# Convolution of a decoder layer: blocks next to the diagonal as three split products, equal pairs squared on ScalarE, the pair products of a unit in two halves

## The chip, the cores and the metric

The kernel runs on one NeuronCore of a Trainium2 chip. Its five engines (TensorE, VectorE, ScalarE, GpSimd, SyncE) run programs of their own and meet at semaphores. The metric is device time in microseconds, lower is better. The kernel before takes 1985.09 us (median of three runs, 1984.59 to 1986.24).

## The reference, cut to what matters

A decoder layer for x of 16 x 256 x 512: attention with a sliding window, then a long convolution mixed with a context, then a sum of eight factor matrices. The change lies in the second part:

```python
kv = jnp.einsum('bhil,bhjl->bijhl', k_, v_)          # k_ and v_ are both the context here
y = irfft(rfft(kv, 1024) * rfft(ssm_kernel, 1024))[..., :512]   # causal convolution along l = 512
out = y + kv * D
out = jnp.einsum('bijhl,bhil->bjhl', out, q_)        # q_: the normalised rows of x
```

Here b runs over 16 batches, h over 32 heads, i and j over the 8 rows of a head, and l over the 512 positions. As k_ and v_ are the same tensor, kv is symmetric in i and j: 36 products of pairs, 8 of them (i = j) squares.

## The kernel before, in words

The convolution is a product with a lower triangular Toeplitz matrix of 512 x 512 for each head (in the kernel's layout the block at distance d under the diagonal is columns d*128 to d*128+127 of a table of shifted taps). One unit is one head and one of two groups of eight batches (BG = 8), 64 units in all (NCU). Its moving matrix has NY = 36 x 8 = 288 columns in each of four chunks of 128 positions (KD = 4). So a unit has ten blocks (c, d) with d <= c: four with c - d = 0, three with c - d = 1, two with 2, one with 3, where c - d picks the chunk of pair products and d the block of taps.

The names: `kk` holds the context of a unit (8 rows for each of 8 batches, four of the rows a second time), loaded by SyncE, two buffers. `kv` holds the 288 products, two buffers; `kv_hi` and `kv_lo` are its rounded part and the rest, `tap_hi` and `tap_lo` the same for the taps. `qs` holds the queries, `y` the result in PSUM (two halves of four banks), `terms` and `res` the sums over i. Units 6 to 57 are "split" (`ALONE = 6`): in them the four blocks with c = d are computed as three matmuls (hi*hi, hi*lo, lo*hi, line 1244) in the reduced float32 form; all other blocks are one float32 matmul in the source, which stands in the trace as two instructions (line 1246).

What each engine does for units in the convolution part, in program order and with lines of the profile:

- SyncE: `kk` of unit u (L1105) waits for the pair products of unit u - 2 (`kv_ready`). The taps of a head (L1114, and L1117 for the split forms) are loaded once for the two units of a head, into one of two buffers, and wait for `conv_done` of the head two before.
- GpSimd, round u: the pair products of unit u + 2 in two operations (L1159, all four chunks of distances 0 to 3; L1161, the pairs at distance 4), behind `kk_landed` and `conv_done` of unit u; then the last sum of unit u - 1 (L1183), then `kv_lo` of unit u + 2 (L1176).
- ScalarE, round u: the queries of unit u + 1 (L1201, L1202), the cast to `kv_hi` of unit u + 2 (L1172), then the result of unit u - 1 back into the big buffer (L1207).
- TensorE: unit u (L1244, L1246) waits for taps, `kv_ready`, `kv_lo_ready`, and for `one_added` of unit u - 2, because the result goes to the same half of PSUM.
- VectorE: unit u (L1280, L1283, L1285, L1290, then the dependent sums L1298, L1301, L1304 that end in `one_added`) waits for `qs_ready`, `res_ready` of unit u - 2 and `conv_done` of unit u.

All orders are written out in the source; there is no scheduler.

## Time and profile before

| what | us |
|---|---|
| median of three runs | 1985.09 |
| the profiled execution's own time | 1984.65 |
| its span | 1982.9 |
| attention part (until about) | 1545 |
| convolution units 6 to 57, first to last VectorE start | 1578.07 to 1825.03 |
| last part (factors), from about | 1857 |

The page gives busy time by engine; the views used further below are the chain of work that ended last, the engines in order of time, the groups of instructions of a stretch, and the busy time by stretches. TensorE's granted clock was 0.996 of full over the whole span. A line of the chain says on which engine and line the end of the program hung in that piece of time.

### The profile page before, as it was taken

How to read it: one execution, taken by the hardware profiler on the slowest of the kernel's cores; microseconds unless marked ns; L12 is line 12 of the kernel's file. 1: busy time of each engine (PE TensorE's matmuls, PEld its weight loads, DVE VectorE, ACT ScalarE, POOL GpSimd, SP SyncE). 2: the span in 40 equal slices, each digit the busy share in tenths (PEclk: the TensorE clock that was granted, in tenths of full speed). 3: DMA queues.
4: the chain of work that ended last, by engine and by line, in shares of the span. 5: the costliest groups of instructions: out<-in, count | busy, mean ns of one | idle time of the engine just before them, and what ended most of it. 6: DMA issues, size and time to landing. Idle time of an engine off the chain costs nothing.

```text
span 1982.9 us, 45446 instructions
## 1 busy us (share of the span) xinstructions
PE 1930.0 (97%) x15708; PEld 1610.9 (81%) x15708; DVE 1547.7 (78%) x4948; ACT 954.6 (48%) x3534; POOL 866.7 (44%) x1000
## 2 busy tenths in 40 slices
PE   6899999999999999999999999999999999999899
PEld 6688888888888888888888888888886788887687
DVE  6777777777777777777777777777777799999887
ACT  4554555555555555555555555555554233333333
POOL 4444334333433343333333333333332588887554
PEclk9999999999999999999999999999999999999999
DMA  6147211111112122121111111111105655554333
GB/s 216 44 121 148 69 54 55 64 54 55 55 55 73 47 97 76 55 80 71 55 55 54 55 55 54 55 56 64 55 33 200 169 118 118 115 113 100 109 141 121
DMA packets 75828, 167.59 MB, mean 85 GB/s; under 512 B 7120, under 2 KB 19536, under 8 KB 75472
## 3 DMA queue, kind: packets, MB, share of 16 engines
q1 hardware_dynamic: 67008, 147.84, 23.7%
q0 software_dynamic: 3840, 8.39, 2.3%
q10 hardware_dynamic: 4752, 8.46, 1.1%
q8 instruction: 127, 2.08, 0.4%
q14 instruction: 101, 0.83, 0.1%
HBM read 114.08 MB, written 50.58 MB: 83 GB/s over the span
## 4 chain that ended last, share of the span: by engine, by line
PE 85%; DVE 9%; issue 2%; ACT 2%; POOL 1%; DMA 1%; DVEq 0%; SPq 0%; ACTq 0%; POOLq 0%
PE banks L542 22%; PE banks L604 18%; PE banks L581 9%; PE banks L557 9%; PE banks L1246 7%; PE banks L567 6%; PE banks L535 5%; PE banks L1474 5%; PE banks L1244 3%; DVE terms L1280 1%; ACT pr L681 1%; DVE banks L1298 1%; DVE banks L1290 1%; PE banks L492 1%; DVE terms L1301 1%
## 5 line engine op out<-in xcount | busy, mean ns | idle before, releaser
L681 ACT ACTIVATE pr<-pr,mx 128x128 f32<-128x128 f32 x1024 | 399.1, 391 | 354.3 <-DVE mx L905 354.3
L763 POOL TENSOR_TENSOR m<-m,rope_sb 128x512 f32<-128x512 f32 x160 | 206.5, 1291 | 512.7 <-ACT m L668 512.7
L542 PE MATMUL banks<-xTh,wh 128*128 128x256 f32 x1280 | 375.8, 294 | 2.3 <-DVE xTl L865 1.4
L542 PE MATMUL banks<-xTl,wh 128*128 128x256 f32 x1280 | 362.5, 283 | 0.0
L542 PE MATMUL banks<-xTh,wl 128*128 128x256 f32 x1280 | 362.0, 283 | 0.0
L914 DVE TENSOR_TENSOR den<-ac,es 128x4 f32<-128x4 f32 x256 | 51.6, 202 | 253.4 <-ACT es L684 253.3
L542 PEld LDWEIGHTS banks<-xTh,wh 128*128 128x128 f32 x1280 | 245.6, 192 | 4.2 <-issue 1.8
L542 PEld LDWEIGHTS banks<-xTl,wh 128*128 128x128 f32 x1280 | 246.0, 192 | 0.0
L542 PEld LDWEIGHTS banks<-xTh,wl 128*128 128x128 f32 x1280 | 245.2, 192 | 0.0
L1246 PE MATMUL banks<-kv,tap 128*128 128x288 f32 x864 | 238.4, 408 | 2.1 <-DMA tap<-padded_taps 1.5
L905 DVE CUSTOM_DVE_ANT_0 pr<-banks,mask_sb 128x128 f32<-128x128 f32 x1024 | 234.8, 283 | 0.2
L780 POOL TENSOR_TENSOR sk<-mx,sink_sb 128x4 f32<-128x4 f32 x256 | 59.8, 233 | 383.4 <-DVE mx L905 383.3
L581 PE MATMUL banks<-pT,vv 128*64 128x256 f32 (+1 forms) x2048 | 223.1, 339 | 1.7 <-DVE oTl L936 1.7
L604 PE MATMUL banks<-woh,oTh 128*128 128x512 f32 x512 | 220.5, 431 | 0.4 <-DVE x L949 0.4
L668 ACT ACTIVATE m<-banks,bqk_sb 128x256 f32<-128x256 f32 x320 | 134.2, 470 | 163.7 <-PE banks L542 163.4
L557 PE MATMUL banks<-kT,qT 32*128 32x128 f32 (+1 forms) x4096 | 203.8, 335 | 3.2 <-DVE mx L905 2.4
L581 PEld LDWEIGHTS banks<-pT,vv 128*64 128x64 f32 x2048 | 124.7, 136 | 97.8 <-issue 43.2
L604 PE MATMUL banks<-woh,oTl 128*128 128x512 f32 x512 | 200.9, 392 | 0.0
L604 PE MATMUL banks<-wol,oTh 128*128 128x512 f32 x512 | 200.8, 392 | 0.0
L881 DVE SCALAR_TENSOR_TENSOR m<-banks,bqk_sb,rope_sb 128x256 f32<-128x256 f32 x320 | 139.8, 478 | 77.5 <-ACT m L668 72.3
L919 DVE TENSOR_TENSOR pr<-pr,rden 128x512 f32<-128x512 f32 x256 | 188.2, 735 | 8.8
L681 ACT ACTIVATION_READ_ACCUMULATOR pr<-pr,mx 128x1 f32 x1024 | 191.3, 187 | 0.0
(120 smaller groups left out, 4192.4 us busy)
## 6 DMA issues: line engine op xcount, KB each, us to landing
kk<-in_ctxt SPq DMA_DIRECT2D x64, 192.0 KB, 3.6
x_in<-in_x SPq DMA_DIRECT2D x16, 512.0 KB, 3.5
xt_split<-xTh SPq DMA_DIRECT2D x16, 512.0 KB, 2.7
xt_split<-xTl SPq DMA_DIRECT2D x16, 512.0 KB, 4.0
xb<-in_x SPq DMA_DIRECT2D x16, 512.0 KB, 4.2
factors<-in_factors POOLq DMA_DIRECT2D x8, 1024.0 KB, 8.6
x_part_rows<-x SPq DMA_DIRECT2D x16, 512.0 KB, 3.0
xTh<-xt_split SPq DMA_DIRECT2D x16, 512.0 KB, 4.8
```

Source lines behind the costliest of these rows:

```text
L542: last = pe.matmul(bank[:, h * T:(h + 1) * T], w[:, n, c, h * P:(h + 1) * P], a[:, s, c, :], start=(c == 0 and i == 0), stop=(c == KD - 1 ...
L557: last = pe.matmul(sP[:, r, t * P:P + 2 * t * P], qT[rr, p % 2, h, t * P:(t + 1) * P], kT[rr, kslot, h, 0:(t + 1) * P], start=(h == 0), st ...
L567: last = pe.transpose(pP[:, (2 * a + t) * P:(2 * a + t + 1) * P], pr[:, (2 * p + 2 + j) % 4, a, t * P:(t + 1) * P], id_sb[:])
L581: last = pe.matmul(vP[a * HD:(a + 1) * HD, k * P:T], vv[:, (u // 4) % 2, k, g * HD:(g + 1) * HD], pT[:, s, a, 2 * k * P:2 * P + k * P], st ...
L604: last = pe.matmul(oP[:], a[:, o, c, t * P:(t + 1) * P], w[:, c, :], start=(c == 0 and n == 0), stop=(c == NO - 1 and n == 2))
L668: last = act.activation(m2[:, s, 1 - half], bank[:, half * T:(half + 1) * T], ACT.Identity, bias=bqk_sb[:, y.sweep, i, half:half + 1])
L681: act.activation(pr[:, s, a, cols], pr[:, s, a, cols], ACT.Exp, bias=mx[:, s, i:i + 1], scale=-1.0, accum_out=ac[:, s, i:i + 1])
L763: pool.tensor_tensor(m2[:, s], m2[:, s], rope_sb[:, 1 if i == 0 else 0, 1:3], ALU.mult).then_inc(sin_ready, 1)
L881: last = dve.scalar_tensor_tensor(m1[:, s, half], bank[:, half * T:(half + 1) * T], bias[:, half:half + 1], tab[:, 0], ALU.add, ALU.mult)
L905: last = dve.tensor_tensor_reduce(pr[:, s, a, t * P:(t + 1) * P], sP[:, 2 * j + a, 2 * t * P:(2 * t + 1) * P], mask_sb[:, t * P:(t + 1) * ...
L919: dve.tensor_tensor(quarters, quarters, rden[:, s].unsqueeze(2).broadcast_to([P, 2 * NT, P]), ALU.mult).then_inc(pn_ready, 1)
L1246: last = pe.matmul(y[:, s, c, 0:NY], tap[:, k, block], kv[:, s, c - d, :], start=(d == 0), stop=(d == c))
```

## The change

In split units the three blocks with c - d = 1 are computed in three split matmuls too. For this `kv_hi` and `kv_lo` hold chunks 0 and 1 instead of chunk 0 alone, so the cast on ScalarE and the subtraction on GpSimd have 576 columns instead of 288. Chunks 0 and 1 of `kv` are then read by no matmul. The pair products of a split unit are made in four operations on GpSimd, two for chunks 0 and 1 (`half` 0) and two for chunks 2 and 3 (`half` 1), and the pairs at distance 0 are left out there; ScalarE makes them as squares of `kk`, in two operations. Half 0 of unit u + 2 waits for no `conv_done` where unit u is split. The whole taps that are loaded for a split head shrink from 384 to 256 columns. `pT` of the attention part moves into the space of the pairs, which doubles.

GpSimd, the products of unit 8 and what follows them, before (kk the context, kv the products, res the last sum of unit 5):

```order
L1159 TENSOR_TENSOR kv<-kk 128x4x256 [waits conv_done,kk_landed0]
L1161 TENSOR_TENSOR kv<-kk 128x4x32
L1183 TENSOR_TENSOR res<-terms 128x256 [waits res_placed,one_added]
L1176 TENSOR_TENSOR kv_lo<-kv,kv_hi 128x288 [waits kv_hi_ready]
L1159 TENSOR_TENSOR kv<-kk 128x4x256 [waits conv_done,kk_landed1]
```

and in the changed kernel:

```order
L1189 TENSOR_TENSOR kv<-kk 128x2x192 [waits kk_landed0]
L1191 TENSOR_TENSOR kv<-kk 128x2x32
L1189 TENSOR_TENSOR kv<-kk 128x2x192 [waits conv_done,kk_landed0]
L1191 TENSOR_TENSOR kv<-kk 128x2x32
L1229 TENSOR_TENSOR res<-terms 128x256 [waits res_placed,one_added]
L1222 TENSOR_TENSOR kv_lo<-kv,kv_hi 128x576 [waits kv_hi_ready]
```

The two operations of 1024 and 128 elements a partition became four of 384 and 64, the first two without `conv_done`; `kv_lo` doubled in size.

ScalarE, the round that casts `kv_hi` of unit 8, before:

```order
L1201 COPY qs<-queries 128x4x64 [waits q_landed1,terms_ready]
L1202 COPY qs<-queries 128x4x32
L1172 CAST kv_hi<-kv 128x288 [waits kv_ready]
L1207 COPY queries<-res 128x4x8x8 [waits q_landed0,res_ready]
L1201 COPY qs<-queries 128x4x64 [waits q_landed0,terms_ready]
```

and in the changed kernel:

```order
L1250 COPY qs<-queries 128x4x64 [waits q_landed1,terms_ready]
L1251 COPY qs<-queries 128x4x32
L1205 ACTIVATE kv<-kk 128x2x64 [waits kv_lo_ready,kk_landed0]
L1217 CAST kv_hi<-kv 128x576 [waits conv_done,kv_first_ready,kv_square_ready]
L1205 ACTIVATE kv<-kk 128x2x64 [waits conv_done]
L1256 COPY queries<-res 128x4x8x8 [waits q_landed0,res_ready]
```

Two squares (ACTIVATE) stand around the cast, which is twice as wide and now waits for the first half of the products, the first squares and `conv_done` instead of `kv_ready`.

TensorE, the start of unit 6 (output chunks 0, 1 and a part of 2), before:

```order
L1244 MATMUL banks<-kv_hi,conv_tap_hi 128x288 [waits kv_lo_ready,one_added,kv_ready,tap_landed0]
L1244 MATMUL banks<-kv_lo,conv_tap_hi 128x288
L1244 MATMUL banks<-kv_hi,conv_tap_lo 128x288
L1246 MATMUL banks<-kv,tap 128x288
L1244 MATMUL banks<-kv_hi,conv_tap_hi 128x288
L1244 MATMUL banks<-kv_lo,conv_tap_hi 128x288
L1244 MATMUL banks<-kv_hi,conv_tap_lo 128x288
L1246 MATMUL banks<-kv,tap 128x288 x2
```

and in the changed kernel:

```order
L1294 MATMUL banks<-kv_hi,conv_tap_hi 128x288 [waits kv_equal_ready,kv_lo_ready,one_added,kv_ready,tap_landed0]
L1294 MATMUL banks<-kv_lo,conv_tap_hi 128x288
L1294 MATMUL banks<-kv_hi,conv_tap_lo 128x288
L1294 MATMUL banks<-kv_hi,conv_tap_hi 128x288
L1294 MATMUL banks<-kv_lo,conv_tap_hi 128x288
L1294 MATMUL banks<-kv_hi,conv_tap_lo 128x288
L1294 MATMUL banks<-kv_hi,conv_tap_hi 128x288
L1294 MATMUL banks<-kv_lo,conv_tap_hi 128x288
L1294 MATMUL banks<-kv_hi,conv_tap_lo 128x288
L1297 MATMUL banks<-kv,tap 128x288
```

The single float32 block of output chunk 1 became three split matmuls, and one of the two float32 blocks of output chunk 2 as well. Over a unit, 12 split and 6 float32 matmuls became 21 and 3.

The diff:

```diff
--- before.py
+++ after.py
@@ -99,7 +99,7 @@
         self.fsum = self.tables + 6 * T + 2 * GS * HD
         self.probs = self.fsum + KD * D
         self.pairs = self.probs + 8 * T
-        words = self.pairs + 4 * NY
+        words = self.pairs + 8 * NY
         ctx.enter_context(nc.sbuf_tensor("arena", [P, words], F32))
         self.base = nc.sbuf_base - 4 * words
         self.id_sb = ctx.enter_context(nc.sbuf_tensor("id_sb", [P, P], F32))
@@ -157,7 +157,7 @@
     ac = sb("ac", [P, 4, 2 * NT])
     den = sb("den", [P, 4, 2 * NT])
     rden = sb("rden", [P, 4, 2 * NT])
-    pT = sb("pT", [P, 2, 2, SK])
+    pT = space.at("pT", space.pairs, 2, 2, SK)
     xb = sb("xb", [P, NT, D])
     x1 = sb("x1", [P, NT, D])
     x1n = xn
@@ -1046,8 +1046,8 @@
     terms = space.at("terms", space.moving + 5632, 2, KD, 5 * 8 * BG)
     tap_hi = space.at("conv_tap_hi", space.probs, 2, D, dt=F32R)
     tap_lo = space.at("conv_tap_lo", space.probs + 2 * D, 2, D, dt=F32R)
-    kv_hi = space.at("kv_hi", space.pairs, 2, NY, dt=F32R)
-    kv_lo = space.at("kv_lo", space.pairs + 2 * NY, 2, NY, dt=F32R)
+    kv_hi = space.at("kv_hi", space.pairs, 2, 2, NY, dt=F32R)
+    kv_lo = space.at("kv_lo", space.pairs + 4 * NY, 2, 2, NY, dt=F32R)
     big = space.queries
     y = space.banks[:].rearrange("p (s c) n -> p s c n", s=2)
 
@@ -1056,6 +1056,9 @@
     kk_landed = [sem(f"kk_landed{i}") for i in range(2)]
     tap_landed = [sem(f"tap_landed{i}") for i in range(2)]
     kv_ready = sem("kv_ready")
+    kv_first_ready = sem("kv_first_ready")
+    kv_equal_ready = sem("kv_equal_ready")
+    kv_square_ready = sem("kv_square_ready")
     kv_hi_ready = sem("kv_hi_ready")
     kv_lo_ready = sem("kv_lo_ready")
     qs_ready = sem("qs_ready")
@@ -1102,6 +1105,8 @@
     def load_contexts(sp, u):
         bg, h, s = where(u)
         wait(sp, kv_ready, u - 1)
+        if split(u - 2):
+            sp.wait_ge(kv_equal_ready, u - 2 - ALONE + 1)
         sp.dma_start(kk[:, s], ctx_in[bg, h]).then_inc(kk_landed[s], 16)
 
     def load_taps(sp, u):
@@ -1110,7 +1115,7 @@
             return
         if g > 1:
             sp.wait_ge(conv_done, opening[g - 1])
-        whole = D - P if split(u) else D
+        whole = D - 2 * P if split(u) else D
         sp.dma_start(tap[:, g % 2, 0:whole], diagonals(0, h, whole)).then_inc(tap_landed[g % 2], 16)
         if split(u):
             for i, part in ((1, tap_hi), (2, tap_lo)):
@@ -1148,19 +1153,57 @@
             for b in {4: (12, 13), 5: (14,), 6: (15,)}.get(u, ()):
                 load_queries(sp, b)
 
+    def contexts(u):
+
+        k0 = kk[:, u % 2, :, 0:8, :].rearrange("p c i b -> p c (i b)")
+        row = k0.ap[1][0]
+
+        def later(first, apart, count, half):
+            c = 2 * half if half is not None else 0
+            n = KD if half is None else 2
+            return bass.AP(tensor=k0.tensor, offset=k0.offset + c * row + first * BG,
+                           ap=[list(k0.ap[0]), [row, n], [BG, count], [1, 8 * BG]])
+
+        return k0, later
+
     def pairs(pool, u):
         s = u % 2
         pool.wait_ge(kk_landed[s], 16 * (u // 2 + 1))
         wait(pool, conv_done, u - 1)
         n = 8 * BG
-        k0 = kk[:, s, :, 0:8, :].rearrange("p c i b -> p c (i b)")
-        row = k0.ap[1][0]
-        shifted = bass.AP(tensor=k0.tensor, offset=k0.offset, ap=[list(k0.ap[0]), [row, KD], [BG, 4], [1, n]])
+        k0, later = contexts(u)
         pool.tensor_tensor(kv[:, s, :, 0:4 * n].rearrange("p c (d n) -> p c d n", d=4),
-                           k0.unsqueeze(2).broadcast_to([P, KD, 4, n]), shifted, ALU.mult)
+                           k0.unsqueeze(2).broadcast_to([P, KD, 4, n]), later(0, 1, 4, None), ALU.mult)
         pool.tensor_tensor(kv[:, s, :, 4 * n:NY],
                            kk[:, s, :, 0:4, :].rearrange("p c i b -> p c (i b)"),
                            kk[:, s, :, 4:8, :].rearrange("p c i b -> p c (i b)"), ALU.mult).then_inc(kv_ready, 1)
+
+    def unequal_pairs(pool, u, half):
+
+        s, c = u % 2, slice(2 * half, 2 * half + 2)
+        pool.wait_ge(kk_landed[s], 16 * (u // 2 + 1))
+        if half or not split(u - 2):
+            pool.wait_ge(conv_done, u - 1)
+        n = 8 * BG
+        k0, later = contexts(u)
+        pool.tensor_tensor(kv[:, s, c, n:4 * n].rearrange("p c (d n) -> p c d n", d=3),
+                           k0[:, c].unsqueeze(2).broadcast_to([P, 2, 3, n]), later(1, 1, 3, half), ALU.mult)
+        pool.tensor_tensor(kv[:, s, c, 4 * n:NY],
+                           kk[:, s, c, 0:4, :].rearrange("p c i b -> p c (i b)"),
+                           kk[:, s, c, 4:8, :].rearrange("p c i b -> p c (i b)"),
+                           ALU.mult).then_inc(kv_ready if half else kv_first_ready, 1)
+
+    def equal_pairs(act, u, half):
+
+        s, c = u % 2, slice(2 * half, 2 * half + 2)
+        if not half:
+            act.wait_ge(kk_landed[s], 16 * (u // 2 + 1))
+        if not half and split(u - 2):
+            act.wait_ge(kv_lo_ready, u - 2 - ALONE + 1)
+        else:
+            act.wait_ge(conv_done, u - 1)
+        last = act.activation(kv[:, s, c, 0:8 * BG], kk[:, s, c, 0:8, :].rearrange("p c i b -> p c (i b)"), ACT.Square)
+        last.then_inc(kv_equal_ready if half else kv_square_ready, 1)
 
     def first_pairs(pool, u):
         if u == 0:
@@ -1168,12 +1211,15 @@
         pairs(pool, u)
 
     def pairs_high(act, u):
-        act.wait_ge(kv_ready, u + 1)
-        act.copy(kv_hi[:, u % 2], kv[:, u % 2, 0, :]).then_inc(kv_hi_ready, 1)
+        equal_pairs(act, u, 0)
+        act.wait_ge(kv_first_ready, u - ALONE + 1)
+        wait_apart(act, conv_passed, (kv_square_ready, u - ALONE + 1), (conv_done, u - 1))
+        act.copy(kv_hi[:, u % 2], kv[:, u % 2, 0:2, :]).then_inc(kv_hi_ready, 1)
+        equal_pairs(act, u, 1)
 
     def pairs_low(pool, u):
         pool.wait_ge(kv_hi_ready, u - ALONE + 1)
-        pool.tensor_tensor(kv_lo[:, u % 2], kv[:, u % 2, 0, :], kv_hi[:, u % 2].bitcast(F32),
+        pool.tensor_tensor(kv_lo[:, u % 2], kv[:, u % 2, 0:2, :], kv_hi[:, u % 2].bitcast(F32),
                            ALU.subtract).then_inc(kv_lo_ready, 1)
 
     def last_sum(pool, u):
@@ -1184,7 +1230,10 @@
 
     def gpsimd(pool):
         for u in range(NCU):
-            if u + 2 < NCU:
+            if split(u + 2):
+                unequal_pairs(pool, u + 2, 0)
+                unequal_pairs(pool, u + 2, 1)
+            elif u + 2 < NCU:
                 pairs(pool, u + 2)
             if u > 0:
                 last_sum(pool, u - 1)
@@ -1231,6 +1280,7 @@
         pe.wait_ge(kv_ready, u + 1)
         if split(u):
             pe.wait_ge(kv_lo_ready, u - ALONE + 1)
+            pe.wait_ge(kv_equal_ready, u - ALONE + 1)
         wait(pe, one_added, u - 1)
         for c in range(KD):
             if u == 1 and c == KD - 1:
@@ -1239,9 +1289,10 @@
                 pe.wait_ge(x1t_evac, 2 * B)
             for d in range(c + 1):
                 block = slice(d * P, (d + 1) * P)
-                if c == d and split(u):
+                if c - d < 2 and split(u):
                     for n, (a, b) in enumerate([(tap_hi, kv_hi), (tap_hi, kv_lo), (tap_lo, kv_hi)]):
-                        last = pe.matmul(y[:, s, c, 0:NY], a[:, k, block], b[:, s], start=(d == 0 and n == 0), stop=(n == 2))
+                        last = pe.matmul(y[:, s, c, 0:NY], a[:, k, block], b[:, s, c - d], start=(d == 0 and n == 0),
+                                         stop=(d == c and n == 2))
                 else:
                     last = pe.matmul(y[:, s, c, 0:NY], tap[:, k, block], kv[:, s, c - d, :],
                                      start=(d == 0), stop=(d == c))
```

## Rows read from the trace of the kernel before

**Rows 1.** The page: span, then busy time, share of the span and instructions.

```profile
span 1982.9 us, 45446 instructions
...
PE 1930.0 (97%) x15708; PEld 1610.9 (81%) x15708; DVE 1547.7 (78%) x4948; ACT 954.6 (48%) x3534; POOL 866.7 (44%) x1000
```

**Rows 2.** Busy us by engine in stretches, granted clock, DMA share, GB/s.

```profile
core 0: us, PE busy (x) PEld busy (x) DVE busy (x) ACT busy (x) POOL busy (x), PEclk, DMA share, GB/s
...
1574.00:1578.00 4.00, 4.00 (x16) 3.22 (x16) 0.36 (x1) 1.66 (x4) 3.43 (x4) 0.69 0.47 105
1600.00:1650.00 50.00, 48.66 (x249) 40.16 (x248) 47.16 (x73) 19.52 (x43) 42.75 (x43) 1.00 0.48 114
```

**Rows 3.** Chain that ended last, 1601 to 1622 us: start, duration, what.

```profile
1602.21 0.63 PE banks L1244 x3
1602.85 0.49 PE banks L1246 x2
1603.34 0.39 PE banks L1244 x3
...
1606.55 0.41 PE banks L1244 x3
...
1607.08 1.23 DVE terms L1280
...
1611.75 0.14 issue
1611.89 0.63 PE banks L1244 x3
```

**Rows 4.** Groups, 1600 to 1820 us: shapes, count | busy, mean ns | idle before.

```profile
...
L1159 POOL TENSOR_TENSOR kv<-kk 128x1024 f32<-128x1024 f32 x46 | 103.8, 2257 | 33.0 <-PE banks L1244 33.0
...
L1176 POOL TENSOR_TENSOR kv_lo<-kv,kv_hi 128x288 fp32r<-128x288 f32 x46 | 36.9, 802 | 0.0
...
L1183 POOL TENSOR_TENSOR res<-terms 128x256 f32<-128x256 f32 x46 | 33.7, 732 | 0.0
...
L1161 POOL TENSOR_TENSOR kv<-kk 128x128 f32<-128x128 f32 x46 | 21.1, 460 | 0.0
...
L1172 ACT CAST kv_hi<-kv 128x288 fp32r<-128x288 f32 x46 | 19.9, 432 | 123.9 <-POOL kv L1161 123.9
...
L1202 ACT COPY qs<-queries 128x128 f32<-128x128 f32 x46 | 18.9, 411 | 0.0
```

**Rows 5.** GpSimd in order of time, one unit: start, duration, what.

```profile
1602.05 2.26 POOL L1159 TENSOR_TENSOR kv<-kk 128x1024 f32<-128x1024 f32 x1 [0.51 <-PE banks L1244]
...
1605.36 0.81 POOL L1176 TENSOR_TENSOR kv_lo<-kv,kv_hi 128x288 fp32r<-128x288 f32 x1
1607.09 2.25 POOL L1159 TENSOR_TENSOR kv<-kk 128x1024 f32<-128x1024 f32 x1 [0.92 <-PE banks L1244]
```

**Rows 6.** VectorE in order of time: first op of four units, idle before.

```profile
1578.07 1.23 DVE L1280 TENSOR_TENSOR terms<-banks,qs 128x1024 f32<-128x1024 f32 x1 [3.71 <-PE banks L1244]
...
1582.65 1.22 DVE L1280 TENSOR_TENSOR terms<-banks,qs 128x1024 f32<-128x1024 f32 x1
...
1587.74 1.23 DVE L1280 TENSOR_TENSOR terms<-banks,qs 128x1024 f32<-128x1024 f32 x1 [0.43 <-PE banks L1244]
...
1825.03 1.22 DVE L1280 TENSOR_TENSOR terms<-banks,qs 128x1024 f32<-128x1024 f32 x1 [0.45 <-PE banks L1244]
```

**Rows 7.** SyncE's queue from 1600 us, and the landing of L1105's 64 loads.

```profile
1602.78 0.43 SPq L1117 DMA_DIRECT2D conv_tap_lo<-padded_taps  x1
1604.74 5.37 SPq L1105 DMA_DIRECT2D kk<-in_ctxt  x2
...
DMA to landing us min/median/max: 2.1/3.6/7.4
```

**Rows 8.** TensorE in order of time: the first split unit's start.

```profile
1571.52 0.40 PE L1244 MATMUL banks<-kv_hi,conv_tap_hi 128*128 128x288 f32 x1 [1.98 <-DMA conv_tap_lo<-padded_taps]
```

**Rows 9.** GpSimd at the end of the attention part.

```profile
1516.01 2.25 POOL L1159 TENSOR_TENSOR kv<-kk 128x1024 f32<-128x1024 f32 x1
...
1518.64 2.71 POOL L1159 TENSOR_TENSOR kv<-kk 128x1024 f32<-128x1024 f32 x1
```

## The prediction

> **What bounds the kernel now.** I read the page first. TensorE is busy for 97% of the span, VectorE for 78% [rows 1]. That mean says nothing of the stage that changes, so I asked for stretches. Between 1600 and 1650 us, inside the split units, TensorE is busy 48.66 of 50 us, VectorE 47.16, GpSimd 42.75, ScalarE 19.52, at a granted clock of 1.00 [rows 2]. Three engines are nearly full, so which one ends a unit has to be read from the chain.
>
> The chain [rows 3] alternates. A TensorE unit starts at 1602.21, VectorE's unit on its result at 1607.08, and the next TensorE piece on the chain at 1611.89, after 0.14 us of issue behind VectorE's end. That TensorE unit is two units later, since it waits for the PSUM half that VectorE has just given back. So two units take 1611.89 - 1602.21 = 9.68 us, or 4.84 a unit: 4.87 from TensorE's start to VectorE's (matmuls and handoff) plus 4.81 from VectorE's start to TensorE's (VectorE's unit, 4.67, and the 0.14). The VectorE starts of units 6 and 57 give the same from afar: (1825.03 - 1578.07) / 51 = 4.842 us [rows 6].
>
> Neither engine alone takes as long. VectorE's starts at 1578.07 and 1582.65 are only 4.58 apart, back to back without a wait, and the next, at 1587.74, comes after 5.09 us, 0.43 of it waiting for TensorE [rows 6]. So VectorE by itself could run a unit in about 4.59, and the loop through both is what costs 4.84.
>
> **The change, part by part.**
>
> *TensorE.* A unit loses three float32 blocks and gains three split triples. On the chain a float32 block (two instructions) takes 0.49 and a triple 0.39 to 0.41 away from the unit's start [rows 3]. The 0.63 at the start of a unit is a triple with the pipeline filling, and that is paid once in either kernel. The gain is 3 x (0.488 - 0.398) = 0.27 us a unit, where 0.488 and 0.398 are the middles of these rows. Bounds: 3 x (0.49 - 0.39) = 0.30 above. Below, if every triple cost the 0.63, 3 x (0.49 - 0.63) = -0.42; I take 0.27, since the triples inside the unit are the nearest rows, and there one already follows a float32 block each time. One more semaphore is waited for at the unit's start, but the last to arrive is still VectorE's.
>
> *The loop.* A TensorE unit stands once in a loop of two units, so the period falls by half of that: (9.684 - 0.27) / 2 = 4.707 us a unit. VectorE's own 4.59 lies below, so it doesn't take over. Between the VectorE starts of units 6 and 57 lie 51 periods: 51 x 0.135 = 6.9 us. Unit 6 itself starts when its taps have landed, behind 1.98 us of idle TensorE [rows 8]; it stands on the chain in full, so its 0.27 comes on top. Sum on TensorE and VectorE: -7.2 us.
>
> *GpSimd.* This is the engine that gets work. Before, a round is four operations of 1024, 128, 256 and 288 elements, mean 2257, 460, 732 and 802 ns [rows 4]. From the first two a rate follows: (2257 - 460) / 896 = 2.006 ns an element, with 0.203 us fixed. A round now has two of 384 elements (0.203 + 0.770 = 0.973 each), two of 64 (0.331 each), the last sum (0.732) and `kv_lo` of 576 (0.802 + 288 x 2.006 ns = 1.380). That is 4.72 us of durations. They overlap a little: before, four operations of 2.26 + 0.46 + 0.74 + 0.81 = 4.27 run from 1602.05 to 1606.17, in 4.12 [rows 4, 5], 0.05 for each joint. Six joints give 4.72 - 0.30 = 4.42. The lower bound is this 4.42. The upper is no overlap and a handoff of 0.13 exposed (the chain's TensorE piece ends at 1606.96 [rows 3], GpSimd starts at 1607.09 [rows 5]) at one of its waits: 4.85. I take 4.45, because the durations in these rows are steady and GpSimd now starts half 0 of the next unit ahead of `conv_done`, so that the handoff falls in a time when it has work. 4.45 is below 4.707, so GpSimd follows with 0.26 us to spare. Its `kv_lo` ends about 0.13 + 0.97 + 0.33 + 0.73 + 1.38 - 0.15 = 3.4 us after `conv_done` of unit u and is needed 4.7 after it, so a late round costs nothing unless it is late every time.
>
> [...]
>
> *ScalarE.* A round gains two squares of 128 elements and 288 more columns of cast. The rows give 432 ns for a cast of 288 and 411 for a copy of 128 [rows 4]; at most the additions are 0.43 + 2 x 0.41 = 1.25 us, at least 0.5 (a cast at half the rate and the squares hidden in overlaps). The engine is busy 19.52 of 50 us [rows 2], 1.9 a unit, so 3.1 at the most of 4.7. Cast and last squares are done by 0.13 + 0.86 + 0.41 = 1.4 us after `conv_done`, and GpSimd comes to `kv_lo` only about 2.0 after it. Behind the waiting cast are queued the second squares, the result of the unit before and the queries of the one after next; the last are due in two units. I cost it at nothing. If that cover went, GpSimd's `kv_lo` would move by the same amount, and 1.3 us of slack lie behind it.
>
> *SyncE and the loads.* `kk` of unit u + 2 may be issued when half 1 is done, about 1.3 us after `conv_done` instead of 2.7 (1604.74 against 1602.05 [rows 5, 7]). The new need is 3.3 us after the next `conv_done`, a period earlier than before less that. Lead before: 2 x 4.84 - 2.7 = 7.0; lead now: 4.7 + 3.3 - 1.3 = 6.7 us. Landing takes 3.6 in the median and 7.4 at worst [rows 7]; it now follows the taps (last issue 1602.78 + 0.43) at once rather than 1.5 us later, so it will take longer than the median. The worst row, if it came every time, would cost 0.7; I take 0. The taps are 128 columns shorter, a gain of nothing to 0.2 us at unit 6.
>
> *Start.* Unit 7's products begin late in any case, and its round is 0.3 us longer (4.42 against 4.12). It is not on the chain. I charge 0.2.
>
> *Sum.* -7.2 + 0.2 = -7.0 us against the profiled execution's own time, 1984.65, that is 1977.65. That execution is 0.44 below the median of the runs, so the forecast for the median is 1978.1.
>
> **The rivals.**
>
> *A. GpSimd ends the unit, but below 4.84.* If overlaps and handoffs come out near the upper bound, the period is 4.72 to 4.84 instead of 4.707: 4.78 gives 51 x 0.062 = 3.2 us saved, 1981.9. For it: GpSimd is busy 42.75 of 50 us before any work is added, and the chain will leave it 5% of idle time. Against: it waited 33.0 us for TensorE before L1159 in 46 rounds, 0.72 a round [rows 4], and the addition is 0.3.
>
> *B. GpSimd's round passes 4.84 and the kernel is slower.* Place: the four product operations beside VectorE's. Price: at the end of the attention part the same L1159 took 2.71 instead of 2.25 us once [rows 9]. One such stretch of 0.46 in each round gives 4.45 + 0.46 = 4.91, and 51 x 0.07 = 3.6 us more: 1988.7. It decides from 4.84 a round. Against: in the convolution part the mean over 46 is 2257 ns, so nothing stretches it there now. The Trainium skill, "SBUF — State Buffer", names an exclusive port pair that a VectorE operation with two SBUF inputs and a GpSimd operation take from each other; VectorE's operations in this part each read one input from PSUM, so by the page B would not happen, and the row without stretch agrees.
>
> *C. The time stays.* VectorE sets the unit after all: from 1607.08 to 1611.75 it took 4.67, and with 0.14 behind it 4.81. Then only 0.03 x 51 = 1.5 us go: 1983.6. Against: the 4.58 between two starts in [rows 6].
>
> *D. The loads of `kk` are late* behind the taps by some 0.3 us in each second unit: 26 x 0.3 = 7.8 us back, which gives 1985.9, no gain. Against: no wait of that kind is in [rows 4].
>
> *E. More than forecast.* The clock fell to 0.69 in 1574 to 1578 us [rows 2], between its levels of 1.2 and 2.4 GHz, after the idle 1.98 us before unit 6 [rows 8]. A shorter wait could leave it up: 4 us at 0.69 is 1.2 us lost, so 1976.9. If VectorE alone were the bound at 4.59, the floor is 51 x 0.25 = 12.8 us: 1972.3. I give that little.
>
> **How the numbers follow.** Forecast 0.66, A 0.13, B 0.06, C 0.06, D 0.04, E 0.05. What a measurement of this kernel can tell from no change is 0.2%, or 4.0 us: faster means below 1981.1. The forecast and E lie there, and about half of A: 0.66 + 0.05 + 0.07 = 0.78. Same is the other half of A, C and half of D and of B: 0.06 + 0.06 + 0.02 + 0.02 = 0.16. Slower is what is left, 0.06. The range, 1975.3 to 1982.6, takes in the TensorE saving between 0.20 and 0.30 a unit, the start's uncertainties, the clock of E, and most of A.
>
> **What would show it right or wrong.** After: the chain still alternates TensorE and VectorE, with the two-unit loop at 9.41; TensorE's unit on it is shorter by 0.27; 51 periods take 240.1 us instead of 246.96. GpSimd's four product operations take 0.97, 0.33, 0.97, 0.33 and `kv_lo` 1.38, and it still waits for TensorE before the second half. VectorE's waits for TensorE shrink to about 0.1 a unit. It would be wrong if GpSimd stood on the chain in the split units, if TensorE waited for `kv_lo`, or if VectorE's single operations were longer than the 1.22 to 1.23 us of L1280 in [rows 6].

## The result and the profile after

| | median us | range | runs |
|---|---|---|---|
| before | 1985.80 | 1984.59 to 1986.41 | 8 |
| after | 1979.07 | 1978.61 to 1980.47 | 8 |

The ratio is 0.9968, with a 95% interval of 0.9958 to 0.9978. The profiled execution of the changed kernel took 1978.86 us with a span of 1976.9, against 1984.65 and 1982.9 before: 6.0 us less in the span, while the medians differ by 6.73. The forecast was 1978.1 for the median, with 7.0 less in the profiled execution, and a range of 1975.3 to 1982.6.

The page: span, and busy time by engine with its share of the span.

```profile
span 1976.9 us, 46176 instructions
PE 1919.7 (97%) x15864; PEld 1614.4 (82%) x15864; DVE 1547.2 (78%) x4948; ACT 993.4 (50%) x3638; POOL 892.7 (45%) x1104
```

TensorE is still "97% busy", as in [rows 1], and nothing in this line tells that the kernel is faster. What changed stands in the stretches. The columns are busy us of TensorE, weight loads, VectorE, ScalarE and GpSimd, then granted clock, DMA share and GB/s.

```profile
core 0: us, PE busy (x) PEld busy (x) DVE busy (x) ACT busy (x) POOL busy (x), PEclk, DMA share, GB/s
1570.00:1574.00 4.00, 1.67 (x13) 1.57 (x12) 3.93 (x7) 0.76 (x3) 0.64 (x1) 1.00 0.99 339
1574.00:1578.00 4.00, 2.89 (x18) 2.39 (x16) 1.33 (x3) 1.68 (x5) 3.81 (x6) 1.00 0.36 92
1600.00:1650.00 50.00, 47.50 (x289) 41.91 (x288) 47.81 (x75) 27.39 (x65) 49.31 (x65) 1.00 0.47 110
```

Against [rows 2], in the same 50 us TensorE has 47.50 instead of 48.66, VectorE 47.81 instead of 47.16, and GpSimd has gone from 42.75 to 49.31: it looks like the bound now, and experiments 3 and 4 below show that it just isn't. In 1574 to 1578 us the clock stayed at 1.00, where it had fallen to 0.69.

The chain that ended last, inside the split units: start, duration, what.

```profile
1607.12 0.14 issue
1607.26 1.43 PE banks L1294 x9
1608.69 0.48 PE banks L1297 x2
1609.17 0.80 PE banks L1294 x6
1609.97 0.97 PE banks L1297 x4
1610.94 0.81 PE banks L1294 x6
1611.75 0.03 issue
...
1611.87 1.23 DVE terms L1331
...
1616.11 0.43 DVE terms L1355
1616.55 0.14 issue
```

It has the shape of [rows 3]: a TensorE unit behind a VectorE unit behind a TensorE unit, joined by 0.14 and 0.12 us. From the TensorE start at 1607.26 to the next on the chain, 1616.55 + 0.13 = 1616.68, is 9.42 us for two units, where it was 9.68 (0.13 is the issue time between VectorE's end and TensorE's start). TensorE's piece, 1607.26 to 1611.75, is 4.49 instead of 4.75. The nine-matmul row at its start is the three triples of output chunks 0 and 1.

VectorE in order of time, the first operation of units 6, 7, 8, 9 and 57, to set against [rows 6].

```profile
1577.50 1.23 DVE L1331 TENSOR_TENSOR terms<-banks,qs 128x1024 f32<-128x1024 f32 x1 [2.63 <-POOL res L1229]
...
1583.60 1.22 DVE L1331 TENSOR_TENSOR terms<-banks,qs 128x1024 f32<-128x1024 f32 x1 [1.43 <-ACT qs L1251]
...
1588.19 1.22 DVE L1331 TENSOR_TENSOR terms<-banks,qs 128x1024 f32<-128x1024 f32 x1
...
1593.02 1.23 DVE L1331 TENSOR_TENSOR terms<-banks,qs 128x1024 f32<-128x1024 f32 x1 [0.18 <-PE banks L1294]
...
1819.04 1.23 DVE L1331 TENSOR_TENSOR terms<-banks,qs 128x1024 f32<-128x1024 f32 x1 [0.17 <-PE banks L1294]
```

The starts alternate, 4.59 apart (VectorE's own pace) and then 4.83 (0.18 of it waiting for TensorE). From unit 7 to unit 57 there are 50 periods: (1819.04 - 1583.60) / 50 = 4.709 us. Before it was (1825.03 - 1582.65) / 50 = 4.848. That is 6.94 us saved. Unit 7 itself starts 0.95 later than before (1583.60 against 1582.65), and 0.95 - 6.94 = -5.99 is the whole difference of the spans. Nothing is won or lost behind unit 57.

Most of the 0.95 is older than the split units. VectorE's first operation of unit 1, before and after:

```profile
1546.64 1.22 DVE L1280 TENSOR_TENSOR terms<-banks,qs 128x1024 f32<-128x1024 f32 x1 [0.57 <-PE banks L1246]
```

```profile
1547.37 1.22 DVE L1331 TENSOR_TENSOR terms<-banks,qs 128x1024 f32<-128x1024 f32 x1 [0.56 <-PE banks L1297]
```

The changed kernel's profiled execution is 0.73 late at unit 1 already. This start differs as much between kernels whose programs are the same up to there: experiments 1, 6 and 10 alter the kernel before only behind this point, and their unit 1 starts at 1546.73, 1548.09 and 1548.33. So the start of a later unit is best counted from unit 1 of its own execution. Unit 7 comes 36.01 us behind unit 1 before and 36.23 after: 0.22 later, and not 0.95.

GpSimd in order of time, one round.

```profile
1640.13 1.02 POOL L1189 TENSOR_TENSOR kv<-kk 128x384 f32<-128x384 f32 x1 [0.21 <-PE banks L1294]
1641.11 0.34 POOL L1191 TENSOR_TENSOR kv<-kk 128x64 f32<-128x64 f32 x1
1641.38 0.74 POOL L1229 TENSOR_TENSOR res<-terms 128x256 f32<-128x256 f32 x1
1642.08 1.43 POOL L1222 TENSOR_TENSOR kv_lo<-kv,kv_hi 128x576 fp32r<-128x576 f32 x1
1643.45 1.02 POOL L1189 TENSOR_TENSOR kv<-kk 128x384 f32<-128x384 f32 x1
1644.44 0.32 POOL L1191 TENSOR_TENSOR kv<-kk 128x64 f32<-128x64 f32 x1
1644.72 1.02 POOL L1189 TENSOR_TENSOR kv<-kk 128x384 f32<-128x384 f32 x1
```

A round without a wait is 1644.72 - 1640.13 = 4.59 us here; before, its four operations took 4.12 and a wait of 0.7 followed. Once it has the context of unit 7, GpSimd has no wait in the split units until 1630.71: it is making up for a late start. From the `kv_lo` of unit 8 on, eight rounds take (1618.54 - 1581.93) / 8 = 4.576 us each, so a free round is about 4.57. The 49.31 above has a part of this catching up in it; from 1650 to 1700 us GpSimd is busy 48.97.

The groups of 1600 to 1820 us, GpSimd and the new work of ScalarE: shapes, count | busy, mean ns | idle before.

```profile
...
L1189 POOL TENSOR_TENSOR kv<-kk 128x384 f32<-128x384 f32 x90 | 91.7, 1019 | 4.2 <-PE banks L1294 4.1
...
L1222 POOL TENSOR_TENSOR kv_lo<-kv,kv_hi 128x576 fp32r<-128x576 f32 x46 | 65.8, 1430 | 0.0
...
L1217 ACT CAST kv_hi<-kv 128x576 fp32r<-128x576 f32 x45 | 30.5, 677 | 47.3 <-POOL kv L1191 24.9 <-PE banks L1294 22.4
L1191 POOL TENSOR_TENSOR kv<-kk 128x64 f32<-128x64 f32 x90 | 29.2, 325 | 0.0
L1205 ACT ACTIVATE kv<-kk 128x128 f32<-128x128 f32 x90 | 27.6, 307 | 0.0
```

The idle time before the products fell from 33.0 us [rows 4] to 4.2.

Last, TensorE and GpSimd where the split units begin.

```profile
1572.38 0.40 PE L1294 MATMUL banks<-kv_hi,conv_tap_hi 128*128 128x288 f32 x1 [2.33 <-DMA conv_tap_lo<-padded_taps]
...
1578.99 0.37 PE L1294 MATMUL banks<-kv_hi,conv_tap_hi 128*128 128x288 f32 x1 [2.10 <-issue]
```

```profile
1574.19 1.01 POOL L1189 TENSOR_TENSOR kv<-kk 128x384 f32<-128x384 f32 x1 [3.55 <-DMA kk<-in_ctxt]
...
1577.38 1.40 POOL L1222 TENSOR_TENSOR kv_lo<-kv,kv_hi 128x576 fp32r<-128x576 f32 x1
```

The last row of TensorE is the start of unit 7, after 2.10 us in which it had nothing ready: `kv_lo` of unit 7 ended at 1577.38 + 1.40 = 1578.78. The part on the prediction comes back to this place.

### The profile page after: what moved, and what is told of

It is laid out like the page before. It is cut to its first block, busy times and chain, and to the rows that moved or that the text cites. A ratio compares the mean times of both kernels' runs of the same rounds, so it can differ in the third digit from the quotient of the medians.

```text
span 1976.9 us, 46176 instructions
## 1 busy us (share of the span) xinstructions
PE 1919.7 (97%) x15864; PEld 1614.4 (82%) x15864; DVE 1547.2 (78%) x4948; ACT 993.4 (50%) x3638; POOL 892.7 (45%) x1104
## 4 chain that ended last, share of the span: by engine, by line
PE 85%; DVE 9%; issue 2%; ACT 1%; POOL 1%; DMA 1%; DVEq 0%; SPq 0%; ACTq 0%; POOLq 0%
PE banks L542 22%; PE banks L604 18%; PE banks L581 10%; PE banks L557 9%; PE banks L567 6%; PE banks L1525 5%; PE banks L1297 5%; PE banks L535 5%; PE banks L1294 4%; DVE terms L1331 2%; DVE banks L1349 1%; DVE banks L1341 1%; DVE terms L1352 1%; ACT pr L681 1%; PE banks L492 1%
## 5 line engine op out<-in xcount | busy, mean ns | idle before, releaser
L919 DVE TENSOR_TENSOR pr<-pr,rden 128x512 f32<-128x512 f32 x256 | 188.3, 735 | 8.8
L772 POOL TENSOR_TENSOR qT<-m,m 128x512 f32<-128x512 f32 x128 | 165.1, 1290 | 24.3 <-POOL m L763 12.5
```

The lines of the kernel that those rows point to most:

```text
L772: pool.tensor_tensor(dst, m1[:, s], m2[:, s], ALU.add).then_inc(qr_ready, 1)
L919: dve.tensor_tensor(quarters, quarters, rden[:, s].unsqueeze(2).broadcast_to([P, 2 * NT, P]), ALU.mult).then_inc(pn_ready, 1)
```

## The experiments

Each was timed beside the kernel before, whose median was 1985.20 beside experiments 1 to 4, 1985.03 beside 6 to 9, and 1985.27 beside 5 and 10 to 12. "Period" is the mean distance of VectorE's unit starts from unit 7 to unit 57.

**1. TensorE's part alone.** The kernel before, with the condition of its matmuls changed:

```diff
-                if c == d and split(u):
+                if c - d < 2 and split(u):
...
-                        ... start=(d == 0 and n == 0), stop=(n == 2))
+                        ... start=(d == 0 and n == 0), stop=(d == c and n == 2))
```

> The kernel before, with TensorE's part of the change alone: the three blocks next to the diagonal as three split matmuls each, which read chunk 0's kv_hi and kv_lo also where chunk 1 is meant (that part of the result is left wrong). GpSimd, ScalarE and the loads are as before. Loop theory (two units hang on one TensorE unit plus one VectorE unit, so half of the 0.27 us arrives): 4.71 us a unit, about 6.9 us less than before, ratio 0.9965, the same as the whole change gave or a little better, since unit 7 isn't delayed at the start. GpSimd theory (in the changed kernel GpSimd, busy 49.3 of 50 us, sets the 4.71): with its old work the period falls further, to VectorE's 4.59, 12 us less, ratio 0.994.

1978.21 us (1977.85 to 1978.57), ratio 0.9964 (0.9952 to 0.9977). VectorE's first operation of units 7 and 57:

```profile
1582.37 1.23 DVE L1280 TENSOR_TENSOR terms<-banks,qs 128x1024 f32<-128x1024 f32 x1 [0.88 <-ACT qs L1202]
...
1818.21 1.22 DVE L1280 TENSOR_TENSOR terms<-banks,qs 128x1024 f32<-128x1024 f32 x1 [0.19 <-ACT qs L1202]
```

Period 235.84 / 50 = 4.717. So the whole gain is TensorE's triples, and the rest of the change (halves, squares, cast) brings no time by itself: it only supplies the parts that the triples need. It even costs a little at the start: unit 7 comes 35.64 us behind unit 1 here, and 36.23 in the changed kernel.

**2. The rest alone.** The changed kernel with the old matmuls (its whole taps have 384 columns again, and the float32 blocks with c - d = 1 read chunk 2 of `kv`):

```diff
...
-                if c - d < 2 and split(u):
+                if c == d and split(u):
...
```

> The changed kernel with TensorE's part undone: 12 split and 6 float32 matmuls a unit as before (the float32 blocks with c - d = 1 read chunk 2 of kv, so that part of the result is wrong), all the new work on GpSimd and ScalarE kept. Loop theory: GpSimd's round of about 4.6 us stays hidden behind the 4.84 us of the old loop, so the time is that of before within 2 us, the difference being unit 7 late at the start (up to 1 us). GpSimd theory: the same here, unless its round is over 4.84; then slower by more than 2 us.

1985.62 us (1984.98 to 1986.15), ratio 1.0001 (0.9992 to 1.001); period (1825.39 - 1583.70) / 50 = 4.834. GpSimd is busy 47.74 of 50 us instead of 42.75 and the time stays within the interval: what was added to GpSimd and ScalarE is hidden as long as TensorE and VectorE need 4.83. Unit 7 comes 36.41 us behind unit 1, 0.40 later than before.

**3. Less work for GpSimd.** The products at distance 3 are left out (256 elements an operation, not 384):

```diff
-        pool.tensor_tensor(kv[:, s, c, n:4 * n]...(d=3), ..., later(1, 1, 3, half), ALU.mult)
+        pool.tensor_tensor(kv[:, s, c, n:3 * n]...(d=2), ..., later(1, 1, 2, half), ALU.mult)
```

> The changed kernel with less work on GpSimd: in split units the products at distance 3 are left out (256 instead of 384 elements in each of the two large operations; results wrong). That takes about 0.5 us from GpSimd's round, 4.6 to 4.1. Loop theory: the period stays 4.71 and the time that of the changed kernel, within 1 us, perhaps 0.5 less from the start where unit 7 waits for GpSimd. GpSimd theory: the period falls to VectorE's 4.59, 6 us less than the changed kernel.

1978.65 us (1978.03 to 1979.30), ratio 0.9966 (0.9954 to 0.9978). The stretch and the two starts:

```profile
1600.00:1650.00 50.00, 47.51 (x289) 41.90 (x288) 47.87 (x74) 29.05 (x64) 42.94 (x64) 1.00 0.47 109
```

```profile
1583.49 1.23 DVE L1331 TENSOR_TENSOR terms<-banks,qs 128x1024 f32<-128x1024 f32 x1 [1.39 <-PE banks L1294]
...
1818.91 1.23 DVE L1331 TENSOR_TENSOR terms<-banks,qs 128x1024 f32<-128x1024 f32 x1 [0.17 <-PE banks L1294]
```

GpSimd is back at 42.94 of 50 us and the period is (1818.91 - 1583.49) / 50 = 4.708, as in the changed kernel. An engine at 49.31 of 50 wasn't the bound of the period. At the start it was: unit 7 comes 35.70 us behind unit 1, 0.53 earlier than in the changed kernel, and GpSimd's round before it (1574.64 to 1578.68) took 4.04 instead of 4.59.

**4. A little more work for GpSimd.** One operation of two elements in each round:

```diff
+        if half:
+            src = kk[:, s, 0, 0:1, 0:2]...
+            pool.tensor_tensor(extra[:, s, 0:2], src, src, ALU.mult)
```

> The changed kernel with one more tiny operation (2 elements a partition, into a tile of its own) in each GpSimd round of a split unit. By the fixed part of GpSimd's operations this costs 0.15 to 0.2 us a round, so the round goes from about 4.6 to about 4.78. Loop theory with only 0.1 us of room on GpSimd: the period becomes GpSimd's, 4.78, about 3.5 us slower than the changed kernel, ratio to before 0.9986. GpSimd theory (GpSimd already sets the period): the whole 0.17 arrives, 4.88, 8.7 us slower than the changed kernel. If the idle room that the trace shows were larger than it looks, nothing changes.

1980.10 us (1979.37 to 1980.57), ratio 0.9974 (0.9964 to 0.9984): 1.0 us above the changed kernel.

```profile
1600.00:1650.00 50.00, 47.46 (x287) 41.80 (x285) 48.26 (x74) 26.75 (x65) 50.00 (x76) 1.00 0.47 110
```

```profile
1641.71 1.07 POOL L1190 TENSOR_TENSOR kv<-kk 128x384 f32<-128x384 f32 x1
1642.67 0.26 POOL L1194 TENSOR_TENSOR extra<-kk 128x2 f32<-128x2 f32 x1
1642.82 0.39 POOL L1195 TENSOR_TENSOR kv<-kk 128x64 f32<-128x64 f32 x1
```

GpSimd has no idle time left, and VectorE's starts are even now, 4.72 apart ((1820.06 - 1583.98) / 50 = 4.722): GpSimd sets the pace. The extra operation takes 0.15 from start to start (1642.67 to 1642.82), so without it a free round is 4.72 - 0.15 = 4.57. The expectation was right in kind and three times too large in size: it expected 3.5 us and a round of 4.78, and the round came out at 4.72. 0.013 us a unit is 0.65 us in the whole; the rest of the 1.0 stands at the start (VectorE's unit 7 at 1583.98 instead of 1583.60).

**5. Much more work for GpSimd.** The same place, an operation of 128 elements:

```diff
+            src = kk[:, s, 0:2, 0:8, :]...
+            pool.tensor_tensor(extra[:, s, 0:128]..., src, src, ALU.mult)
```

> The changed kernel with one more GpSimd operation of 128 elements a partition in each round of a split unit (into a tile of its own). By L1161's row in the kernel before it costs 0.41 to 0.42 us from start to start, so the round goes from 4.56 without waits to 4.98. Loop theory with GpSimd's room used up: the period is GpSimd's 4.98, 51 x 0.27 = 14 us slower than the changed kernel, and slower than the kernel before by 7 us (ratio 1.0036): that is rival B of the prediction, with its point of 4.84 passed. If GpSimd's rounds could slip without harm, nothing changes.

1991.29 us (1990.23 to 1991.79), ratio 1.0028 (1.0017 to 1.0039); period (1831.48 - 1584.90) / 50 = 4.932, where the expectation had 4.98, and 12.2 us above the changed kernel, where it had 14. This is rival B's effect made on purpose: past 4.84 a round, the change would have been a loss. The round of the changed kernel is 0.27 away from that point.

**6. All ten blocks as triples** (the kernel before, its matmuls alone):

```diff
-                if c == d and split(u):
+                if split(u):
```

> The kernel before with all ten blocks of a split unit as three split matmuls each, all on chunk 0's kv_hi and kv_lo (six of ten blocks of the result are left wrong). GpSimd and ScalarE as before. Six float32 blocks go, 0.54 us of TensorE a unit, twice as much as in the run of TensorE's part alone. Loop theory: (9.684 - 0.54) / 2 = 4.57 would be below VectorE's own 4.59, so the period is VectorE's, 4.59 to 4.60, and the time 12 us below the kernel before, ratio 0.994. If half of TensorE's saving arrived without a floor, 4.57 and 13.6 us; if TensorE's saving arrived in full, 4.30 and 27 us.

1972.28 us (1971.79 to 1974.87), ratio 0.9938 (0.9925 to 0.995).

```profile
1600.00:1650.00 50.00, 45.85 (x329) 43.62 (x328) 48.86 (x78) 20.22 (x44) 45.15 (x45) 1.00 0.49 120
```

VectorE's period is (1814.69 - 1585.11) / 50 = 4.592 and it has no wait left. TensorE's own share would have given (9.684 - 6 x 0.09) / 2 = 4.57, so VectorE's 4.59 has taken over. That is the floor for a change of the matmuls alone, with VectorE's operations as they are.

**7. Less work for VectorE.** The changed kernel without the operation at L1336 in split units:

```diff
...
-        dve.tensor_tensor(at(n, [n + BG, 4], [1, BG]), ...
+        if not split(u):
+          dve.tensor_tensor(at(n, [n + BG, 4], [1, BG]), ...
...
```

> The changed kernel with one VectorE operation less in each split unit (L1336, 0.20 us from start to start; its products are left out of the result). Loop theory: VectorE stands once in the loop of two units just as TensorE does, so half of 0.20 arrives, (9.42 - 0.20) / 2 = 4.61, 5 us less than the changed kernel, ratio to before 0.994. GpSimd's round without waits is 4.56, just below. If VectorE itself set the unit, the whole 0.20 would arrive until GpSimd's 4.56 stops it, 7.5 us less.

1975.06 us (1973.87 to 1975.63), ratio 0.9947 (0.9935 to 0.9959); period (1815.02 - 1584.61) / 50 = 4.608. The operation takes 0.20 from start to start, and 0.10 a unit arrives: half, by the same rule as TensorE's 0.27. GpSimd is busy 50.00 of 50 us here (1600 to 1650), so it might be GpSimd's pace instead. It isn't: `kv_lo` of units 8 to 36 starts every (1710.96 - 1582.92) / 28 = 4.573 us, while VectorE's units 7 to 34 are (1709.01 - 1584.61) / 27 = 4.607 apart. GpSimd is catching up on its late start, by 0.03 a round. Had the whole 0.20 arrived, the period would have stopped at this 4.57. Of the expected 5 us the median shows 4.0; unit 1 starts 1.15 us later in this profiled execution (1548.52 against 1547.37). The two engines share one loop of two units, and what is taken from either counts once in it.

**8. PSUM given back earlier.** In the changed kernel TensorE waits for the first of the three dependent sums, and the two later sums work in SBUF alone:

```diff
-        wait(pe, one_added, u - 1)
+        wait(pe, three_added, u - 1)
...
-        dve.tensor_tensor(y[:, s, :, 0:3 * n], tt[:, :, 0:3 * n], y[:, s, :, NY:NY + 3 * n],
+        dve.tensor_tensor(tt[:, :, 0:3 * n], tt[:, :, 0:3 * n], y[:, s, :, NY:NY + 3 * n],
...
-        ... tt[:, :, 3 * n:5 * n], y[:, s, :, 0:2 * n],
+        ... tt[:, :, 3 * n:5 * n], tt[:, :, 0:2 * n],
```

> The changed kernel, with VectorE's first sum (L1349) written to SBUF instead of PSUM, so that the two sums behind it read no PSUM and TensorE may start two units later already behind L1349 (it waits for three_added instead of one_added), 1.15 us earlier. Loop theory, if these two operations take as long as before: the loop falls to 8.3 us for two units and no longer decides; VectorE's 4.59 and GpSimd's 4.56 do, 6 us less than the changed kernel. Rival, the exclusive port pair that the Trainium skill's page 'SBUF — State Buffer' describes: these two operations now have two SBUF inputs, so they and GpSimd's operations shut each other out. GpSimd's round has only 0.15 us of room, and 0.69 + 0.42 = 1.1 us of it would be closed in each unit: 5.7 us a unit, about 48 us slower than the changed kernel.

2011.97 us (2007.82 to 2014.73), ratio 1.0132 (1.0118 to 1.0146). VectorE and GpSimd in order of time:

```profile
...
1642.48 0.69 DVE L1352 TENSOR_TENSOR terms<-terms 128x512 f32<-128x512 f32 x1
1642.51 1.53 POOL L1189 TENSOR_TENSOR kv<-kk 128x384 f32<-128x384 f32 x1
1642.78 0.37 PE L1294 MATMUL banks<-kv_hi,conv_tap_hi 128*128 128x288 f32 x1 [0.80 <-DVE terms L1349]
1643.21 1.12 DVE L1355 TENSOR_TENSOR terms<-terms 128x256 f32<-128x256 f32 x1
...
1644.01 0.50 POOL L1191 TENSOR_TENSOR kv<-kk 128x64 f32<-128x64 f32 x1
```

TensorE did start earlier, right behind the first sum. But the last sum takes 1.12 us instead of 0.43, and GpSimd's products beside the two sums take 1.53 and 0.50 instead of 1.02 and 0.32. VectorE's starts are 5.27 apart (1638.98 and 1644.25). The price is 0.7 us a unit on either engine: 0.69 on VectorE's last sum, 0.51 + 0.18 on GpSimd's two operations, and 5.27 against its free round of 4.57. The expectation's rival had 5.7 a unit, since it took both sums as closed to GpSimd; the first of them (L1352) kept its 0.69. The Trainium skill, "SBUF — State Buffer", "Who interferes with whom", has an exclusive port pair that a VectorE operation with two SBUF inputs and a GpSimd operation that reads SBUF take from each other; this trace agrees, and it agrees in the other direction too: in the changed kernel every VectorE operation reads one input from PSUM, and L1331 keeps its 1.22 to 1.23 beside a GpSimd that is busy 49.31 of 50 us.

**9. Another order of loads at the start.** In the changed kernel the split taps of the first split head are loaded right behind the projections' `out_done`, with a semaphore of their own, and queries that are due later go behind them:

```diff
+                load_split_taps(sp, ALONE)
-            for b in {4: (12, 13), 5: (14,), 6: (15,)}.get(u, ()):
+            for b in {4: (12,), 5: (13,), 7: (14, 15)}.get(u, ()):
...
+            pe.wait_ge(split_landed[k], 32 * ((group[u] - ALONE) // 2 + 1))
```

> The changed kernel with another order of loads at the start of the split units, nothing else: the split taps of the first such head are issued right behind out_done, ahead of the queries of batches 12 to 15, and these are spread over later units (12 behind unit 4's loads, 13 behind unit 5's, 14 and 15 behind unit 7's). In the changed kernel TensorE waits 2.33 us for the split taps of unit 6, and 2.10 us later for unit 7's products, whose context had landed 3.55 us after GpSimd was ready for it. If these waits come from the crowd of loads, unit 7's VectorE start moves from 1583.6 to about 1579 to 1581: 2.5 to 4.5 us less than the changed kernel. If the loads are short of bandwidth whatever their order, another load is late instead and the time is that of the changed kernel within 1 us.

1976.47 us (1975.51 to 1977.17), ratio 0.9955 (0.9941 to 0.9968). This is the shortest time of a version that computes everything: 8.6 us below the kernel before, timed beside it, and 2.6 below the changed kernel's median.

```profile
1571.01 0.37 PE L1302 MATMUL banks<-kv_hi,conv_tap_hi 128*128 128x288 f32 x1 [0.49 <-DVE terms L1363]
...
1575.64 0.37 PE L1302 MATMUL banks<-kv_hi,conv_tap_hi 128*128 128x288 f32 x1 [0.16 <-issue]
```

```profile
1580.26 1.22 DVE L1339 TENSOR_TENSOR terms<-banks,qs 128x1024 f32<-128x1024 f32 x1
```

TensorE starts unit 6 at 1571.01 instead of 1572.38 and unit 7 at 1575.64 instead of 1578.99; VectorE's unit 7 starts at 1580.26 instead of 1583.60, and 33.24 us behind unit 1 instead of 36.23. The period is (1815.67 - 1580.26) / 50 = 4.708, untouched.

**10. The same order of loads in the kernel before.**

> The kernel before with only the new order of loads at the start of the split units (the same edit that took 2.6 us from the changed kernel). There TensorE waited 1.98 us for unit 6's split taps, and its clock fell behind that wait. If the gain is that of the waits for the taps and for unit 7's context, unit 7's VectorE start moves from 1582.7 to about 1580.0 to 1580.5, 2 to 3 us less than the kernel before, ratio 0.9987. If it was the longer GpSimd work of the changed kernel that made the start late there, this run gains less than 1 us.

1983.02 us (1982.00 to 1983.46), ratio 0.9987 (0.9979 to 0.9996): -2.2 us. VectorE's unit 7 starts at 1581.21 instead of 1582.65, which is less than expected, but this profiled execution was 1.69 us late at unit 1; unit 7 comes 32.88 us behind unit 1 instead of 36.01. Period 4.846. The start was late for its loads in either kernel. The order gives 2.2 here and 2.6 in the changed kernel, and the two can't be told apart.

**11. Half 0 waits for `conv_done` too** (the changed kernel):

```diff
-        if half or not split(u - 2):
-            pool.wait_ge(conv_done, u - 1)
+        pool.wait_ge(conv_done, u - 1)
```

> The changed kernel without the early start of half 0: it waits for conv_done of unit u like half 1 does, so GpSimd makes the four product operations after that point, as before the change. GpSimd's round of 4.56 then always begins 0.13 us behind conv_done and kv_lo is its last piece, ready 4.7 us after conv_done. TensorE's starts of units lie 4.59 and 4.83 apart, so each second unit would wait about 0.1 us for kv_lo, but the loop of 9.41 us does not run through that wait on the tight side. Loop theory: the time of the changed kernel within 1.5 us. If the two halves are what hides the GpSimd work: a period of 4.75 to 4.85, 2 to 7 us slower than the changed kernel.

1980.14 us (1979.48 to 1982.09), ratio 0.9974 (0.9964 to 0.9985); period (1820.00 - 1583.63) / 50 = 4.727 instead of 4.709. So the free start of half 0 is worth 0.018 a unit, 0.9 us in all. The medians differ by 1.1 and their ranges overlap, so the size rests on the period, one trace of each.

**12. Experiment 9 with the context of unit 5 loaded ahead of the split taps.**

```diff
-            load(sp, u)
+            if u == 5:
+                load_taps(sp, u)
+            else:
+                load(sp, u)
...
+                load_contexts(sp, 5)
```

> The changed kernel with the new order of loads, and also the context of unit 5 ahead of the split taps and of the queries of batch 12, since in the run with the new order GpSimd still waited 4.52 us for that context and unit 5's VectorE start, at 1566.1, was 1.8 us late. If that wait is the next one on the path: 1 to 1.8 us less than with the new order alone, ratio to before 0.9947. If the loads are short of bandwidth there, the split taps or the queries land late instead and the gain is nothing.

1976.76 us (1976.14 to 1977.24), ratio 0.9955 (0.9943 to 0.9968). Nothing is gained over experiment 9: the products of unit 5 are earlier (1560.96 against 1562.68), but now `kk` of units 6 and 7 lands late (GpSimd waits 2.44 and 1.13 us for it). VectorE's unit 7 starts at 1582.04, which is 33.44 us behind unit 1, where experiment 9 had 33.24. (The start at 1566.1 that the expectation takes for unit 5's is unit 4's.) Of these two orders each only chooses which load is late.

## Why the prediction was right

**TensorE, 0.27 a unit.** It measured 4.75 - 4.49 = 0.26, and experiment 1 shows that it is the whole of the gain.

**The loop of two units, 4.707.** It measured 4.709. The halving is shown from TensorE's side by the change and from VectorE's by experiment 7, and the end of the rule at 4.59 by experiment 6. What the text called 51 periods came to 1819.04 - 1577.50 = 241.54 us instead of 240.1, and the difference lies in its first period, between units 6 and 7, not in the steady ones.

**GpSimd's round, 4.45.** Mis-sized: a free round is 4.57. The overlap was right, but the rate of 2.006 ns an element was that of the widest operation. The changed kernel's own rows give (1019 - 325) / 320 = 2.17 ns, and `kv_lo`, from 802 to 1430 ns for 288 elements more, 2.18. With 0.186 fixed for each operation (325 - 64 x 2.17 ns) a round is 1728 x 2.17 ns + 6 x 0.186 - 6 x 0.05 = 4.57 us. The Trainium skill, "GPSIMD Engine Reference", "Performance versus the Vector engine", states about 2.6 cycles an element for a two-input operation, by an estimate 2.17 ns at the 1.2 GHz that it gives for the engine; the operations of 64 to 576 elements agree. The room to 4.707 was 0.13 and not 0.26, and it held; experiments 3 and 4 stand on the two sides of it. GpSimd did wait for TensorE before its second half, but only each second unit.

**ScalarE at nothing.** Right: two squares of 0.307 and a cast of 0.677 us where 0.432 was, all inside a busy time of 27.39 of 50 us, and experiment 2 costs nothing.

**The loads of `kk` at nothing.** Right in the steady part: no wait for a DMA stands there. Rival D didn't occur.

**Start, 0.2, "it is not on the chain".** This step failed. Up to VectorE's unit 7 the sum had 0.27 and 0.135 saved by TensorE and 0.2 charged, so 0.2 less; counted from unit 1 it measured 0.22 more. TensorE's part came as reckoned: in experiment 1 unit 7 is 36.01 - 35.64 = 0.37 earlier. The charge was too small: the rest of the change costs 0.40 in experiment 2, and 36.23 - 35.64 = 0.59 in the changed kernel. The rows of before that were read too lightly are the `kv_lo` of unit 7 and the matmul that takes it:

```profile
1576.63 0.80 POOL L1176 TENSOR_TENSOR kv_lo<-kv,kv_hi 128x288 fp32r<-128x288 f32 x1
```

```profile
1577.77 0.29 PE L1244 MATMUL banks<-kv_hi,conv_tap_hi 128*128 128x288 f32 x1
```

`kv_lo` was ready at 1577.43, and TensorE, done with unit 6 at a low clock, took it at 1577.77. It was 0.34 us away from the chain, and I had read only that it wasn't on it. In the changed kernel TensorE is done with unit 6 at about 1576.9, 4.5 us after 1572.38 (before, 6.4 after 1571.52 [rows 8]). But `kk` of unit 7 is first used at 1574.19 instead of 1573.33, and the round behind it takes 4.59 instead of 4.10, to 1578.78. The last sum stands in that round too, so that VectorE's unit 6 waits for it (2.63 <-POOL res L1229 in the row at 1577.50) and starts only 0.57 earlier. What the clock gave was spent on waiting. That the longer round is to blame is shown by experiment 3, whose shorter one gives 0.53 back. Experiments 9 and 10 show that the loads set the place as a whole: with earlier split taps VectorE's unit 7 starts at 1580.26.

The miss of 1.0 us in the spans, 7.0 against 5.99, is then 0.73 from before unit 1 and 0.42 from the start, less 0.19 that the 50 periods gave above 50 x 0.135. The 0.73 is no cost of the change as far as the runs show, since unit 1 starts between 1546.64 and 1548.33 without it. It also accounts for all but 0.13 of the 0.86 by which `kk` of unit 7 comes later: SyncE's issues are 0.75 later from the taps at 1554.78 on (1554.03 before). Whether moving `pT` has a share in it wasn't tried by itself. The medians, which don't hang on this one pair of executions, differ by 6.73; but the kernel before has had medians from 1985.03 to 1985.80, so the forecast's last few tenths can't be judged.

**The rivals.** A would have shown a period of 4.72 to 4.84 and evenly spaced starts: experiment 4 has just that, the changed kernel hasn't. B is excluded in the changed kernel by the mean of its product operations, 1019 ns and 325; experiment 5 shows the price of a longer round, and experiment 8 what can stretch GpSimd's operations. The stretched 2.71 in [rows 9] fits that: of VectorE's operations beside it, one (L919, 128x512, at 1518.53) has both inputs in SBUF. C is refuted by experiment 6: VectorE's limit is 4.59. E's clock stayed up, but not for E's reason: the wait before unit 6 was longer, 2.33 against 1.98. In 1574 to 1578 us experiment 1, with the new matmuls in the kernel before, shows 1.00 too, and experiment 2, with the old matmuls in the changed kernel, 0.64. So in these traces it goes with the matmuls, and why they keep the clock up stays open.
